# Order of two TensorE steps in a software-pipelined transformer kernel: products with V ahead of the scores of the same round

## The reference

```python
x = x + 0.5 * ffn(layernorm(x))
x = x + dilated_attn(layernorm(x))
x = x + 0.5 * ffn(layernorm(x))
...
def ffn(x):                                   # the layer that is called twice
    x = conv1d(x, conv_w) + conv_b            # kernel 3 over the tokens
    q, k, v = split(x @ wqkv.T + bqkv)        # 16 heads of 8
    attn = softmax(q @ k.T / sqrt(8))         # 512 x 512 per head
    ctx = attn @ v                            # the "products with V"
    x = layernorm(x + ctx @ wo.T + bo, ln1)
    probs = softmax(x @ gate_w + gate_b)      # 8 experts, all of them computed
    h = relu(x @ w1 + b1)                     # 128 -> 512 for each expert
    return layernorm(x + sum_e probs_e * (h_e @ w2_e + b2_e), ln2)
```

## Time and profile before

| | |
|---|---|
| median of 3 runs | 1551.77 us (1548.29 to 1553.27) |
| the profiled execution's own time | 1550.58 us |
| its span in the profile | 1548.8 us |
| PE busy | 1503.9 us, 97% of the span |
| weight loads of PE | 833.1 us, 54% |
| DVE busy | 1160.9 us, 75% |
| ACT busy | 1122.0 us, 72% |
| POOL busy | 1015.4 us, 66% |
| mean granted clock of TensorE | 0.983 of full speed |

### The profile page before, as it was taken

One profiled execution on the slowest core, in us unless ns is written; L12 is line 12 of the kernel. 1 busy time (PEld: TensorE's weight loads), 2 busy tenths in 40 slices (PEclk: granted clock), 3 DMA queues, 4 the chain that ended last, 5 costly groups with the idle time before them and its releaser, 6 DMA issues.

```text
span 1548.8 us, 26116 instructions
## 1 busy us (share of the span) xinstructions
PE 1503.9 (97%) x8318; PEld 833.1 (54%) x8318; DVE 1160.9 (75%) x1834; ACT 1122.0 (72%) x1636; POOL 1015.4 (66%) x978
## 2 busy tenths in 40 slices
PE   5899999999999999999999999999999999999997
PEld 4434555555555555555555555555555555555476
DVE  4777677878777887777878778777777777767486
ACT  2667777677776777777777776777777777777786
POOL 3533668677676876868677676776767677767342
PEclk7889999999999999999999999999999999999999
DMA  6544223251333415233151332514223241511111
GB/s 167 149 92 114 73 75 91 56 131 43 103 74 85 99 43 129 70 82 91 38 144 50 81 91 61 134 43 126 74 75 98 79 108 43 148 45 36 41 46 31
DMA packets 75310, 130.06 MB, mean 84 GB/s; under 512 B 10614, under 2 KB 39207, under 8 KB 70567
## 3 DMA queue, kind: packets, MB, share of 16 engines
q1 hardware_dynamic: 73894, 124.19, 31.4%
q0 software_dynamic: 1280, 4.20, 1.0%
HBM read 97.42 MB, written 29.62 MB: 82 GB/s over the span
## 4 chain that ended last, share of the span: by engine, by line
PE 86%; DVE 8%; issue 2%; SPq 1%; ACT 1%; DMA 1%; POOL 0%; DVEq 0%; ACTq 0%; POOLq 0%
PE hid_y L1018 16%; PE ctx_ps L1213 15%; PE hid_y L1022 13%; PE hid_y L1019 13%; PE score L1061 12%; DVE negmax L886 3%; PE misc L1018 2%; PE score L1081 1%; PE misc L1153 1%; DVE x1n L350 1%; PE score L1018 1%; PE misc L1110 1%; PE misc L1169 1%; PE misc L1146 1%; PE misc L1022 1%
## 5 line engine op out<-in xcount | busy, mean ns | idle before, releaser
L886 DVE TENSOR_REDUCE negmax<-score 128x2 f32<-128x1024 f32 x484 | 590.4, 1220 | 230.4 <-PE score L1061 230.4
L597 POOL TENSOR_TENSOR hidl<-hid,hidh 128x512 fp32r<-128x512 f32 x456 | 584.8, 1294 | 258.1 <-DVE hidh L843 140.7
L716 ACT ACTIVATE probs<-score 128x1024 f32<-128x1024 f32 x468 | 479.8, 1025 | 108.3 <-PE score L1081 108.1
L745 ACT ACTIVATE hid<-hid_y,cols 128x512 f32<-128x512 f32 x484 | 331.5, 685 | 161.2 <-PE hid_y L1022 150.4
L1213 PE MATMUL ctx_ps<-probs,V 128*18 128x512 f32 x2048 | 272.3, 604 | 2.9 <-DVE ctxT L893 2.8
L1081 PE MATMUL score<-Qp,Kp 32*128 32x512 f32 (+1 forms) x1024 | 266.1, 499 | 0.0
L1061 PE MATMUL score<-Kp,Qp 24*128 24x512 f32 x968 | 244.9, 500 | 15.5 <-DMA Kp<-k_parts_dram 10.7
L1018 PE MATMUL hid_y<-x1h,w1h 128*128 128x512 f32 x484 | 235.9, 487 | 1.5 <-DVE negmax L886 1.3
L370 POOL TENSOR_TENSOR yacc<-yacc,gated 128x512 f32<-128x512 f32 x127 | 171.0, 1347 | 61.7 <-DVE gated L859 61.7
L742 ACT ACTIVATE hidh<-hid_y,cols 128x512 fp32r<-128x512 f32 x256 | 174.8, 683 | 34.6 <-PE hid_y L1022 32.2
L1018 PE MATMUL hid_y<-hidh,w2h 128*128 128x512 f32 x484 | 195.6, 404 | 0.0
(11 more groups left out here) (203 smaller groups left out, 1830.7 us busy)
## 6 DMA issues: line engine op xcount, KB each, us to landing
gate_b<-gate_dram SPq DMA_DIRECT2D x128, 256.0 KB, 3.7
q_parts_dram<-q_parts SPq DMA_DIRECT2D x48, 256.0 KB, 3.0
k_parts_dram<-k_parts SPq DMA_DIRECT2D x48, 256.0 KB, 3.1
Qp<-q_parts_dram SPq DMA_DIRECT2D x64, 192.0 KB
Kp<-k_parts_dram SPq DMA_DIRECT2D x64, 192.0 KB
Qp<-q_parts_dram SPq DMA_DIRECT2D x30, 240.0 KB
Kp<-k_parts_dram SPq DMA_DIRECT2D x30, 240.0 KB
Qp<-q_parts_dram SPq DMA_DIRECT2D x30, 144.0 KB
```

Of the source, the lines that this page charges most:

```text
L597: pool.tensor_tensor(hidl[:, n % RING, :], hid[:, n % 2, :], hidh[:, n % RING, :].bitcast(F32), ALU.subtract).then_inc(s["h_lo"], 1)
L716: act.activation(probs[:, n % 2, 2 * j:2 * j + 2, :], score2[:], ACT.Exp, scale=SCALE)\
L745: act.activation(hid[:, n % 2, :], hid_bank(u, n), ACT.Relu, bias=col(n))\
L886: dve.tensor_reduce(negmax[:, g % 2, :, k % 8], banks_for_max(u.count(32, k))[:], AX.X, ALU.max, negate=True).then_inc(s["a_max"], 1)
```

## The change

The body that makes the products with V becomes a function of its own, `products_with_v`. For units 0 and 1 it is called where it was, at T = 29 + 4n. For units 2 to 15 it is called one tick earlier, at T = 28 + 4n, ahead of `ready_for_max`, `ready_for_probs` and both scores of that round. So in a round with products PE's order for these units is hidden, down, products, scores, where it was hidden, down, scores, products. Waits, operands and the number of instructions are the same. No DMA is moved, and no other engine's list is touched.

```diff
--- before.py
+++ after.py
@@ -46,6 +46,7 @@
 TICKS = 64
 P2_AT = 24
 PV_LAG = 5
+PV_FIRST = 2
 DOWN_LAG = 6
 RING = 4
 GATE_RING = 4
@@ -1088,6 +1089,24 @@
 
                 for _ in range(times):
                     pe.matmul(hid_y[:, 0, 0:128], ident[:], ident[:], start=True, stop=True)
+
+            def products_with_v(u, n):
+                p = u.parity
+                g, kc = divmod(n, TC)
+                wait(pe, s["a_exp"], u.count(32, 2 * n + 2))
+                if n == 0:
+                    wait(pe, s["f_vs"], u.count(1, 1))
+                    wait(pe, s["zero_v"], 1)
+                bank, place = divmod(g, 2)
+                if place == 0 and kc == 0:
+                    wait(pe, s["a_ctx"], u.count(2, bank))
+                for j in range(HG):
+                    half, pair = divmod(j, 2)
+                    last = pe.matmul(ctx_ps[32 * j:32 * j + 2 * VC, :],
+                                     V[p][:, kc, HG * half + 2 * bank + pair, VC * place:VC * place + 2 * VC],
+                                     probs[:, n % 2, 2 * pair + half, :], start=(place == 0 and kc == 0),
+                                     stop=(place == 1 and kc == TC - 1))
+                last.then_inc(s["a_pv"], 1)
 
             pe.wait_ge(s["ident_ready"], 2)
             keep_busy(BUSY[0])
@@ -1182,6 +1201,9 @@
 
                 if T == 63 - TICKS and i0 < 0:
                     pe.wait_ge(s["fills_in"], 32)
+                k = T - P2_AT - PV_LAG + 1
+                if u.n >= PV_FIRST and 0 <= k < 64 and k % HG == 0:
+                    products_with_v(u, k // HG)
                 if 0 <= T < 64 and T % 2 == 0:
                     late = (u.n, T) if T >= P2_AT else (u.n - 1, T + TICKS)
                     if u.n == 0 and T == 2:
@@ -1198,23 +1220,8 @@
                     ready_for_probs(u.n, (T - P2_AT) // 2)
                     scores_for_probs(u.n, (T - P2_AT) // 2)
                 k = T - P2_AT - PV_LAG
-                if 0 <= k < 64 and k % HG == 0:
-                    n = k // HG
-                    g, kc = divmod(n, TC)
-                    wait(pe, s["a_exp"], u.count(32, 2 * n + 2))
-                    if n == 0:
-                        wait(pe, s["f_vs"], u.count(1, 1))
-                        wait(pe, s["zero_v"], 1)
-                    bank, place = divmod(g, 2)
-                    if place == 0 and kc == 0:
-                        wait(pe, s["a_ctx"], u.count(2, bank))
-                    for j in range(HG):
-                        half, pair = divmod(j, 2)
-                        last = pe.matmul(ctx_ps[32 * j:32 * j + 2 * VC, :],
-                                         V[p][:, kc, HG * half + 2 * bank + pair, VC * place:VC * place + 2 * VC],
-                                         probs[:, n % 2, 2 * pair + half, :], start=(place == 0 and kc == 0),
-                                         stop=(place == 1 and kc == TC - 1))
-                    last.then_inc(s["a_pv"], 1)
+                if u.n < PV_FIRST and 0 <= k < 64 and k % HG == 0:
+                    products_with_v(u, k // HG)
 
                 m = T - u.at["experts"]
                 if 0 <= m < 64 and m % 2 == 0:
```

## The result

The changed kernel takes 1569.62 us (median of 4 runs, 1566.65 to 1570.49), the kernel before 1551.13 us in 4 runs of the same session: a ratio of 1.0112, 95% interval 1.0087 to 1.0136, so 1.1% slower. The forecast was 1563 with a range of 1553 to 1573. The profiled execution took 1570.19 us, its span is 1568.4 us, 19.6 more than before, and the granted clock is the same 0.983.

A forecast was written before the change was run, and what follows sets the result against it. PE was taken to set the pace in the middle of the kernel. Terms 0 - 2.1 + 5.6 + 4.6 + 2.8 + 1.6 = 12.5 us, on the profiled 1550.6, gave 1563.1, forecast as 1563, range 1553 to 1573.

The forecast's parts named there:

- The order alone, 0: Each moved group on PE: three changes of kind before and after, 1.74 against 1.75 us, so no cost.
- the rival of hidden weight loads: Weight loads at a change of kind slip under running matmuls: 22 us less, about 1541 with the waits; chance 0.07.
- The ordinary round's cover: Ordinary pairs of rounds: eviction after the later exponential keeps 0.2 us less the signal's way before the hidden matmul.
- The much slower rival: Ordinary rounds lose their cover and hidden matmuls wait 0.1 us in 224 pairs: 22 us, 1585 in all; chance 0.10.
- T = 60, +5.6: Products 8 wait bare for DVE's transpose, with scores queued behind: 0.43 us in 13 units, 5.6 us.
- The 12 places: Idle time of 2.8 us before products, at 0.23 each, taken as 12 places of the wait at T = 60.
- The q projection, +4.6: At t = 38.5 PE waits for DVE's `cl`, made later from the convolution: 0.35 us, 13 times, 4.6 us.
- Two rounds shortened, -2.1: Convolution (t = 36, 13 times) and `m_v` (t = 25, 8 times) join their own kind: 0.10 us each, 2.1 less.
- t = 18, +2.8: Mid batch's exponential delays ACT's eviction, and the hidden matmul waits for its bank: 0.35 us, 8 times, 2.8 us.
- t = 9 to 11.5, +1.6: Later copy `xh` delays DVE's `xl`, for which the `m_q` matmul waits: 0.2 us, 8 times, 1.6 us.
- Four places are not ordinary: Only T = 60, t = 38.5, t = 18 and t = 9 to 11.5 were worked out as places with new waits.

The follow-up runs named there:

- the last run: Kernel before with only the t = 24 products ahead of the scores and DVE's `xl` ahead of the cast: 1551.35 us, ratio 1.0004.
- The run with both groups behind: Changed kernel with product groups 11 and 13 (t = 8 and 16) behind the scores again: 1565.67 us, ratio 1.0103.
- the first experiment: Changed kernel with product groups 2, 8, 11, 13 and 15 behind the scores again: 1559.76 us, ratio 1.0075.
- the run with six groups: Changed kernel with product groups 2, 8, 11, 13, 14 and 15 behind the scores again: 1551.61 us, ratio 0.9997.

## Why the prediction was right, and where not

*The order alone, 0.* Right. The three distances are 0.32, 0.99 and 0.43 against 0.33, 0.98 and 0.44 forecast, the pair lasts 5.04, and ten groups of each unit are free to move. With that the rival of hidden weight loads falls: products to scores is 0.98 in the new company as in unit 0. The first sentence of the Trainium skill that it hung on would have given 22 us of gain. The second says that weight loads overlap running matmuls only where row groups differ ("TensorE: Matmul & The Clock Gate", Part 3, The mechanism). The trace agrees with it at the changes of kind, but not within a kind: there a load of the whole array (0.19, at 802.88 in the kernel before) starts with the whole-array matmul ahead of it, and its own matmul starts 0.23 later. So the sentence can't be taken as it stands for why the loads are bare at a change of kind; that they are is what the distances show.

*The ordinary round's cover.* Right: 0.2 us left and no pair waits. The much slower rival falls.

*T = 60, +5.6.* Right, 6.3: 0.45 instead of 0.43, in 14 units and not 13. (The 12 places worked out before the result were a guess from one wait: the view of waits has 10 such waits before, and the cost came in all 14 units.) The run with group 8 behind gives back 6.0.

*The q projection, +4.6.* The wait is 0.37 in 13 iterations, so 4.9; the growth at the hidden matmul behind is only 0.27, for the reason of the next point.

*Two rounds shortened, -2.1.* The right sign, too small. I counted the distance into the hidden matmuls, 0.33 to 0.23. But the first hidden matmul then has no bare load either, and takes 0.23 instead of 0.34: about 0.2 for each round, not 0.1. The convolution rounds gave 1.2 us before them and 0.11 x 13 = 1.4 after them, the `m_v` rounds 0.7 and 0.8, as the last run shows for `m_v`, where nothing else lies on them. Together 4.1, not 2.1.

*t = 18, +2.8,* was 2.6; *t = 9 to 11.5, +1.6,* was 1.2. The run with both groups behind takes both away.

So the terms that I summed to 12.5 measured 6.3 + 4.9 + 2.6 + 1.2 - 4.1 = 10.9. The forecast fell short by what it left out, 5.0 us at `x1` and 1.6 at the scores of t = 24 (its growth of 0.8, and the 0.7 that `m_v` gives back there), which makes 17.5 of the 17.6. The measured time still lies inside the range, and that is luck in part: the range reached up to 1573 for waits half as large again and for some lost cover in the ordinary rounds, and neither happened; the room was filled by two waits that nobody had forecast. "Four places are not ordinary" was wrong: six groups are. I followed the shift to the readers of the scores and to the steps right behind them, and closed the list there. **DVE's queue carries a shift further.** Through group 15 the maximum of t = 24 comes later in its round, DVE then has, in iterations with a mid batch, eight steps without a gap up to `xl`, and `xl`, which no score feeds, ends 0.48 later for an `x1` that had 0.05 of cover: +5.0. And behind group 14, `msum` and `mwt` delay the maximum of t = 22, a wait of 1.1 us of which the changed kernel shows only about 0.18, since group 15 happens to cover the rest. My first account after the result, that all of the loss sat in the five groups, fell with the first experiment and the one with group 15 behind, and the run with six groups settled it.

What stays open: the 1.6 us before the first hidden matmul. They lie before the first moved group, so I take them for variation between executions; the cause is not shown. The clock doesn't explain them, as the mean granted clock of the first 134 us is 0.85 in both traces (it is 0.83 in the two traces of the study that are latest there, by 2.6 and 3.1). Open is also the spread of the wait at T = 60 between iterations (0.36 to 0.70).

## What to carry to other kernels

When steps of the engine that bounds are reordered at equal cost, the price is not in that engine's sum but in the covers that are swapped: ask for each moved group what was waiting there unseen, and then follow the late readers' own queues for several rounds, to steps that don't read the moved result at all. Such costs don't add: a move can be free only because another one covers its wait, so test the moved places one by one and together. The differences of start times, round by round, against the kernel before find such a place in one table; totals of waits don't.

## What the runs showed of the hardware

A step of DVE can be held until the POOL instruction beside it ends, so its duration depends on when it starts. Here the answers of both traces for `mwt` (128 x 32, two inputs), durations in ns as least, median and greatest of eight:

Before:

```profile
L997 DVE TENSOR_TENSOR mwt<-minv,dil_mask x8: 304/316/334, 277.6 to 934.3; 128x32 f32<-128x32 f32 x8
```

After:

```profile
L998 DVE TENSOR_TENSOR mwt<-minv,dil_mask x8: 835/860/1130, 281.3 to 949.1; 128x32 f32<-128x32 f32 x8
```

The instruction is the same, and POOL is busy beside it in both. In the kernel before it starts at 840.58, POOL's `hidl` ends at 840.84, and `mwt` at 840.89. With group 14 ahead it starts at 848.14, POOL's `yacc` ends at 848.90, and `mwt` at 848.94. In all 14 traces of this study, 112 times in all, `mwt` started while a POOL instruction ran and ended 0.05 us after that instruction's end. The ends tell of a wait for the rest of POOL's instruction and not of slower work, and the shift made it meet the next one. In every kernel with group 14 ahead its median is 0.80 to 0.86, in every one with it behind 0.30 to 0.36; in the one iteration of the changed kernel with 0.36 at t = 26, it met `yacc` earlier and took 1.13. That is 0.5 us of DVE's time in each of eight iterations, from a shift alone.

Other steps of the kernel before do the same: `ctxs` (128 x 256, two inputs) takes 0.42 where no POOL instruction is under way and 1.46 where 1.17 us of one were left, and the cast `hidh` 0.38 and 1.26 with 0.97 left. `xl`, which reads one of its inputs from PSUM, is not held: 0.69 with 0.93 us left, 0.67 with none. The Trainium skill ("GPSIMD Engine Reference", 1. Specifications) says that GpSimd shares its SBUF interfaces with VectorE and that instructions with two SBUF inputs contend. The rows agree for `mwt` and `ctxs`, and show the size: the whole rest of POOL's instruction. No run here moves POOL's step alone. I had taken DVE's durations as fixed when I moved it in time.

The cost of a change of kind on PE shows at both neighbours: from a whole-array matmul to another kind 0.33 instead of 0.23, and 0.34 instead of 0.23 from the first whole-array matmul after a change to the next. A round in which a step joins its own kind saves both.
